# Patch embedding of an audio tower: one fp32 product of normalised patches becomes three fp32r products of raw patches, with the norm applied behind them

## The reference

```python
def layer_norm(x, gamma, beta, eps):
    mu = jnp.mean(x, axis=-1, keepdims=True)
    var = jnp.mean(jnp.square(x - mu), axis=-1, keepdims=True)
    return (x - mu) * jax.lax.rsqrt(var + eps) * gamma + beta

x = layer_norm(x, g1, b1, 1e-6)                # x: (64, 7, 1024)
x = jnp.einsum('bpd,dh->bph', x, W) + b        # W: (1024, 512)
h = layer_norm(x, g2, b2, 1e-6)
h = h + attention(layernorm(h))                # 16 heads of 128
h = h + ffn(layernorm(h))                      # inputs rounded to fp8, 512 x 512
```

## Time and profile before

| | us |
|---|---|
| median of 3 runs | 274.49 |
| lowest and highest | 274.19 and 275.79 |
| the profiled execution | 274.52 |
| its span in the trace | 272.7 |

### The profile page before, as it was taken

One profiled execution on the slowest core, in us unless ns is written; L12 is line 12 of the kernel. 1 busy time (PEld: TensorE's weight loads), 2 busy tenths in 40 slices (PEclk: granted clock), 3 DMA queues, 4 the chain that ended last, 5 costly groups with the idle time before them and its releaser, 6 DMA issues.

```text
span 272.7 us, 3956 instructions
## 1 busy us (share of the span) xinstructions
PE 264.4 (97%) x1506; PEld 225.6 (83%) x1506; DVE 156.6 (57%) x325; ACT 129.5 (47%) x220; POOL 0.2 (0%) x4
## 2 busy tenths in 40 slices
PE   6899999999999999999999999999999999999995
PEld 6434446999999999999999999999999999988963
DVE  4579878555545536264555445363555454578892
ACT  2664952364535443544435344445545354356460
POOL 0000000000000000000000000000000000000000
PEclk9999999999999999999999999999999999999999
DMA  6999000124314040413223040404133100000004
GB/s 169 335 288 394 6 0 1 54 102 154 101 55 154 0 154 0 154 19 135 58 96 132 22 154 0 154 0 154 19 135 95 59 0 0 0 4 0 0 2 135
DMA packets 5444, 23.82 MB, mean 87 GB/s; under 512 B 1019, under 2 KB 1483, under 8 KB 3260
## 3 DMA queue, kind: packets, MB, share of 16 engines
q1 hardware_dynamic: 5436, 23.71, 25.9%
HBM read 22.79 MB, written 0.92 MB: 87 GB/s over the span
## 4 chain that ended last, share of the span: by engine, by line
PE 92%; DVE 3%; DMA 2%; SPq 1%; ACT 1%; issue 1%; DVEq 0%
PE bank L274 15%; PE bank L275 15%; PE bank L276 15%; PE acc L309 10%; PE acc L411 8%; PE bank L387 5%; PE bank L395 5%; PE acc L415 4%; PE bank L401 2%; PE acc L524 2%; PE bank L380 2%; DMA tokw_raw<-tok_w 2%; PE bank L282 2%; PE acc L479 1%; PE acc L494 1%; SPq L228 1%
## 5 line engine op out<-in xcount | busy, mean ns | idle before, releaser
L274 PE MATMUL bank<-ht_hi,qkvw_hi 128*128 128x448 f32 (+2 forms) x204 | 74.7, 366 | 0.5 <-DVE ht_lo L749 0.5
L275 PE MATMUL bank<-ht_lo,qkvw_hi 128*128 128x448 f32 (+2 forms) x204 | 73.3, 359 | 0.0
L276 PE MATMUL bank<-ht_hi,qkvw_lo 128*128 128x448 f32 (+2 forms) x204 | 73.2, 359 | 0.0
L749 DVE TENSOR_TENSOR qkvw_lo<-raw,qkvw_hi 128x1536 fp32r<-128x1536 f32 x16 | 28.1, 1758 | 30.7 <-ACT qkvw_hi L546 30.7
L274 PEld LDWEIGHTS bank<-ht_hi,qkvw_hi 128*128 128x128 f32 x204 | 38.4, 188 | 3.7 <-issue 0.6
L276 PEld LDWEIGHTS bank<-ht_hi,qkvw_lo 128*128 128x128 f32 x204 | 38.3, 188 | 3.3
L275 PEld LDWEIGHTS bank<-ht_lo,qkvw_hi 128*128 128x128 f32 x204 | 38.4, 188 | 3.0
L749 DVE TENSOR_TENSOR z_lo<-bank,z_hi 128x448 fp32r<-128x448 f32 x15 | 9.4, 624 | 43.2 <-ACT z_hi L546 43.2
L309 PE MATMUL acc<-tokw_raw,xt 128*112 128x512 f32 x64 | 29.3, 598 | 0.9 <-DMA tokw_raw<-tok_w 0.9
L546 ACT CAST qkvw_hi<-raw 128x1536 fp32r<-128x1536 f32 x16 | 23.6, 1482 | 0.0
L309 PEld LDWEIGHTS acc<-tokw_raw,xt 128*112 128x112 f32 x64 | 10.6, 176 | 14.1 <-issue 9.6
(11 more groups left out here) (122 smaller groups left out, 355.8 us busy)
## 6 DMA issues: line engine op xcount, KB each, us to landing
raw<-heads_w SPq DMA_DIRECT2D x16, 1024.0 KB, 4.9
tokw_raw<-tok_w SPq DMA_DIRECT2D x4, 512.0 KB, 6.9
x_in<-patches SPq DMA_DIRECT2D x3, 448.0 KB, 8.7
ffnw_raw<-ffn_w SPq DMA_DIRECT2D x1, 1024.0 KB, 18.5
out<-h_sb SPq DMA_DIRECT2D x3, 224.0 KB, 2.3
x_in<-patches SPq DMA_DIRECT2D x2, 224.0 KB, 3.0
g_row<-tok_g SPq DMA_DIRECT2D x1, 224.0 KB, 11.2
b_row<-tok_b SPq DMA_DIRECT2D x1, 224.0 KB, 11.6
```

The costliest lines, as they stand in the source:

```text
L274: nc.tensor.matmul(ps, hi, whi, start=first, stop=False, skip_group_check=True)
L275: nc.tensor.matmul(ps, hi, wlo, start=False, stop=False, skip_group_check=True)
L276: return nc.tensor.matmul(ps, lo, whi, start=False, stop=last, skip_group_check=True)
L749: return nc.vector.tensor_tensor(dst, src, hi.bitcast(F32), ALU.subtract)
```

## The change

The transposes now take the raw patches. With s the standard deviation of a row and m its mean, the normalised product is (x·g1)W/s - (m/s)·(g1 W) + b1 W + b. The second norm doesn't care about a factor common to a row, so the kernel computes s times that: (x·g1)W - m·(g1 W) + s·(b1 W + b), and adapts the epsilon of the next norm.

- `patch_full` brings the raw transposed block out times g1 (`x_full`, on DVE for tiles 0 and 1, on ACT for tiles 2 and 3), `patch_hi` casts it on ACT, and the low part is taken on DVE for tiles 0 and 1 and on GpSimd for tiles 2 and 3.
- The weights are split: `split_tokw` casts each piece on ACT, `tokw_lo_part` takes the low part on GpSimd. `embed` issues three fp32r products where there was one in fp32.
- Two spare columns of tile 0's patches hold g1 and b1, so that rows 112 and 113 of `acc[0]` become g1 W and b1 W (+ b, added by `gains_done`). They are split into `gain_rows` (`gains_hi`, `gains_lo`).
- The row statistics (-m and s) of two tiles at a time go into `stat_cols`, are transposed (`stat_transposes`) and split into `stat_t`, and one product a tile, `recentre`, adds them and ends the tile (`tok_ps`).
- The unpaired Newton iterations are gone: each inverse root starts from a square root on ACT (`token_root`, `stream_root`). The low part of the first head's weights moves from DVE to GpSimd. `tokw_raw` now lies in the two slots of `raw`, so that the heads' first loads wait for the last low part of the weights, and `x_full` lies in `ffnw_raw`.

```diff
@@ SP: loads
+            load_tokw(0)
             load(x_in[:, 1, :], patches[1], x_landed[1])
-            load_tokw(0)
...
+            sp.wait_ge(tokw_lo_ok, len(TOKW_PIECES))
             for s in range(2):
                 sp.dma_start(raw[:, s, :], heads_w[s]).then_inc(raw_landed[s], 16)
+            sp.wait_ge(x_lo_late_ok, 4)
             sp.dma_start(ffnw_raw[:], ffn_w).then_inc(ffnw_landed, 16)
@@ PE
+            def embed(t, piece):
+                a, b = TOKW_PIECES[piece]
...
+                pe.wait_ge(x_hi_ok, 2 * t + half + 1)
+                pe.wait_ge(tokw_hi_ok, piece + 1)
+                for k in range(a, b):
+                    nc.tensor.matmul(acc[t][0:m, :], xt_hi[:, t, k, 0:m], tokw_hi[:, k, :], start=(k == 0),
+                                     stop=False, skip_group_check=True)
...
+                for k in range(a, b):
+                    nc.tensor.matmul(acc[t][0:m, :], xt_lo[:, t, k, 0:m], tokw_hi[:, k, :], start=False,
+                                     stop=False, skip_group_check=True)
+                pe.wait_ge(tokw_lo_ok, piece + 1)
+                for k in range(a, b):
+                    nc.tensor.matmul(acc[t][0:m, :], xt_hi[:, t, k, 0:m], tokw_lo[:, k, :], start=False,
+                                     stop=False, skip_group_check=True)
+            def gains_done():
+                pe.wait_ge(tok_b_lo_ok, 1)
+                nc.tensor.matmul(acc[0][0:SPARE, :], bias_row[:], tok_b_split[:], start=False, stop=False,
+                                 skip_group_check=True).then_inc(gain_ps, 1)
+            def recentre(t):
+                pe.wait_ge(gain_lo_ok, 1)
+                pe.wait_ge(stat_lo_ok, t // 2 + 1)
+                nc.tensor.matmul(acc[t][0:TR, :], stat_t[:, t, :], gain_rows[:], start=False, stop=True,
+                                 skip_group_check=True).then_inc(tok_ps, 1)
...
+            embed(0, 0)
+            embed(0, 1)
+            patch_transposes(1)
+            embed(0, 2)
+            embed(1, 0)
+            embed(0, 3)
+            gains_done()
+            stat_transposes(0)
+            patch_transposes(2)
+            embed(1, 1)
+            recentre(0)
+            embed(1, 2)
+            patch_transposes(3)
+            embed(1, 3)
+            recentre(1)
+            stat_transposes(1)
+            for piece in range(4):
+                embed(2, piece)
+            recentre(2)
+            stream_transposes(0)
+            embed(3, 0)
+            embed(3, 1)
+            stream_transposes(1)
+            embed(3, 2)
+            embed(3, 3)
+            recentre(3)
             stream_transposes(2)
@@ ACT
-            take_root(0)
-            normalise(0, slice(IN_DIM // 2, IN_DIM))
...
+            patch_hi(0, 0)
+            patch_hi(0, 1)
+            split_tokw(0)
+            split_tokw(1)
+            patch_hi(1, 0)
+            patch_hi(1, 1)
+            split_tokw(2)
+            split_tokw(3)
...
@@ GpSimd
+            tokw_lo_part(0)
+            tokw_lo_part(1)
+            tokw_lo_part(2)
+            tokw_lo_part(3)
+            b = slice(B_LO, B_LO + 1)
+            pool.wait_ge(tok_b_hi_ok, 1)
+            pool.wait_ge(tokw_lo_ok, len(TOKW_PIECES))
+            lo_part(tok_b_split[b], tok_b_raw[b], tok_b_split[b]).then_inc(tok_b_lo_ok, 1)
+            pool.wait_ge(tok_b_lo_ok, 1)
+            for t in range(2, TILES):
+                for half in range(2):
+                    patch_lo(t, half)
+            pool.wait_ge(qkvw_hi_ok, 1)
+            lo_part(qkvw_lo[0][:].rearrange("p a k e -> p (a k e)"), raw[:, 0, 0:QKV],
+                    qkvw_hi[0][:].rearrange("p a k e -> p (a k e)")).then_inc(qkvw_lo_ok, 1)
@@ DVE
+            patch_full(0, 0)
+            patch_full(0, 1)
+            patch_lo(0, 0)
+            patch_lo(0, 1)
+            patch_moments(0)
+            patch_full(1, 0)
+            patch_full(1, 1)
+            patch_lo(1, 0)
+            patch_lo(1, 1)
+            patch_moments(1)
+            patch_sigmas(0)
+            patch_moments(2)
+            stat_lo(0)
+            patch_moments(3)
+            gains_lo()
+            patch_sigmas(1)
             dve.wait_ge(rows_landed, 32)
-            stream_norms(0, None, patch=(3, patch_moments(3)))
-            stream_norms(1, 0)
-            stream_norms(None, 1, between=lambda i: split_qkv(0, 0) if i == 0 else None)
-            stream_norms(2, None, between=lambda i: stream_lo(0) if i == 0 else None)
-            stream_norms(None, 2)
-            stream_lo(1)
-            stream_norms(3, None, between=lambda i: stream_lo(2) if i == 0 else None)
-            stream_norms(None, 3)
+            stream_norms(0, between=lambda: stat_lo(1))
+            stream_norms(1, between=lambda: stream_lo(0))
+            stream_norms(2, between=lambda: stream_lo(1))
+            stream_norms(3, between=lambda: stream_lo(2))
             stream_lo(3)
```

More of the change, by code:

```diff
@@ L288, in patch_transposes @@
                     pe.wait_ge(ident_landed, 16)
-                    pe.wait_ge(x0_half_normed, 1)
-                else:
[L291 to L315, removed]
+                pe.wait_ge(x_landed[t], 16)
@@ new lines, in patch_full, with split_tokw @@
+            def patch_full(t, half):
+                act.wait_ge(xt_ps, 2 * t + half + 1)
+                act.wait_ge(x_lo_ok, 2 * (t - 2) + half + 1)
+                for k in range(half * HALF, (half + 1) * HALF):
+                    last = nc.scalar.mul(x_full[:, t % 2, k, :],
+                                         bank[2 * (t % 2) + half][:, k % HALF * TR:(k % HALF + 1) * TR],
+                                         g1_col[:, k:k + 1])
+                last.then_inc(x_full_ok, 1)
+            def split_tokw(i):
+                a, b = TOKW_PIECES[i]
+                act.wait_ge(tokw_landed[i], 16)
+                hi_part(tokw_hi[:, a:b, :], tokw_raw[:, a:b, :]).then_inc(tokw_hi_ok, 1)
@@ new lines, in gains_hi, with token_root @@
+            def gains_hi():
+                act.wait_ge(gain_ps, 1)
+                for row in (G_ROW, G_AGAIN):
+                    hi_part(gain_rows[row:row + SPARE - G_ROW, :], acc[0][G_ROW:SPARE, :]).then_inc(gain_hi_ok, 1)
+            def token_root(t):
+                c = TILES + t
+                act.wait_ge(tok_var_ok, t + 1)
+                act.wait_ge(x_eps_ok, t // 2 + 1)
+                nc.scalar.activation(root[:, c:c + 1], moments[:, c, 1:2], ACT.Sqrt, bias=x_eps_4[:, t:t + 1],
+                                     scale=4.0).then_inc(tok_root_ok, 1)
@@ L571, in normalise_stream, with stream_root @@
+            def stream_root(t):
+                c = 2 * TILES + t
+                act.wait_ge(h_var_ok, t + 1)
+                nc.scalar.activation(root[:, c:c + 1], moments[:, c, 1:2], ACT.Sqrt, bias=eps_4[:, 1:2],
+                                     scale=4.0).then_inc(h_root_ok, 1)
             def normalise_stream(t):
@@ new lines, in moments_of, with rsqrt_from_root @@
+                nc.vector.bn_aggr(moments[:, c, :], stats[:, c, 0:len(parts), :]).then_inc(done, 1)
+            def rsqrt_from_root(c, minus_v4):
+                v, y, n = vscaled[:, c:c + 1], rstd[:, c:c + 1], newton[:, c:c + 1]
+                link(nc.vector.reciprocal(y, root[:, c:c + 1]))
+                need(minus_v4)
+                link(nc.vector.scalar_tensor_tensor(out=n, in0=y, scalar=v, in1=y, op0=ALU.mult, op1=ALU.mult))
+                link(nc.vector.scalar_tensor_tensor(out=y, in0=n, scalar=3.0, in1=y, op0=ALU.add, op1=ALU.mult))
```

387 lines of the change are left out of this document (220 added, 167 removed).

## The result

The changed kernel takes 289.67 us (median of 4 runs, 286.26 to 290.13), against 274.71 for the kernel before beside it (274.19 to 275.79). The ratio is 1.050, with a 95% interval from 1.046 to 1.054; the quotient of the two medians alone is 1.054. The profiled execution took 290.13 us, with a span of 288.3: 15.6 more than the 272.7 before.

A forecast was written before the change was run, and what follows sets the result against it. PE bounded the kernel before; after the change, queues of GpSimd, ACT and DVE would. S at 29.8 plus 23.75 puts Q at 53.6 against 45.06, so 274.5 + 8.5 = 283 us, range 278 to 289.

The forecast's parts named there:

- PE's work: Ahead of the head loop: products cost 24.4 us instead of about 31, 6.6 less, but PE doesn't stay the bound.
- S: Start of DVE's norms of tile 0, forecast at 29.8 us against 20.5 before.
- steps 1 to 3: Ahead of S: tile 0's start, GpSimd's low parts of pieces 0 and 1, then pieces 2, 3 and bias up to `recentre`.
- Step 1: PE's warm-up ends at 5.85 us, tile 0's transposes start there; PE's first product stays at 9.4, nothing won.
- From S to Q: Norm pairs one tile at a time on DVE, with waits for ACT's roots of 1.4 and 0.9 us: 23.75 us.
- Q: Start of the first head's queries and keys, forecast at 53.6 us against 45.06; everything behind it unchanged.
- Its own signs of being wrong: First statistics of `acc[0]` before 24 us, DVE's waits on GpSimd showing in the norms, or a differing head loop.
- GpSimd at DVE's pace: Rival on GpSimd's low parts: each piece costs 1.22 us less, S 25.9, Q 49.7, 279 us; chance 0.16.
- No change: Rival on the path to Q: S near 24 with no waits on ACT, 273 to 277 us; chance 0.07.
- faster: Rival: the norms start as early as before, at 20.5 us, Q 41.9, 271.3 us; chance 0.07.
- Exclusion: Rival: DVE operations with two SBUF inputs wait for a whole GpSimd operation; Q 57.8, 287 us; chance 0.22.
- clock: Rival: PE's idling drops it to 1.2 GHz, 3.7 us behind Q, up to 2 before S; 288 us; chance 0.10.

The follow-up runs named there:

- e2: The changed kernel with products of ones that nobody reads in PE's gaps: 285.69 us, 1.040 of the kernel before.
- e1: The changed kernel with GpSimd's low part of the first head's weights cut into 12 instructions of 128x128: 287.14 us, 1.044 of the kernel before.
- e8: The changed kernel with all engines' orders rewritten, fillers, and every low part of weights and bias on DVE: 273.99 us, 0.9955 of the kernel before.
- e10: e8 with each of GpSimd's four late low parts of the patches as four instructions of 128x112: 273.38 us, 0.9934 of the kernel before.
- e7: The changed kernel with all engines' orders rewritten and fillers, GpSimd keeping three of four weight pieces: 280.02 us, 1.016 of the kernel before.

## Why the prediction was right, and where its size was off

The direction held: slower, by 5%. The range held only just: over the 274.5 of before, 278 to 289 is 1.013 to 1.053, and the ratio of 1.050 lies inside, but the median of 289.67 stands 0.7 us above its upper end. The single value of 283 was 5 to 7 us short.

- **PE's work, and that it is not the bound**: right at the full clock. The products cost 0.23 us each there, and PE was idle for 2.6, 2.5 and 5.4 us ahead of its waits. The gain of 6.6 us on PE shows nowhere. At half the clock PE did become the bound for a time, from 22.66 to 28.8 us.
- **The path to S**, steps 1 to 3: right in GpSimd's prices (2.35 for 2.44, 1.27 for 1.37, 3.48 for 3.5) and, with the clock held (e2), in its last links over GpSimd and the bias to the gains. As the kernel ran, PE's slow products had taken the place of GpSimd's second piece and of the bias. S was 4.1 us later. Step 1 took the start of the warm-up from the earlier trace rows and missed that `ones_ok` is now raised by GpSimd, which costs 0.5 us; the warm-up itself took 0.9 longer, and its length, from 4.69 to 5.57 us between executions, is explained by no edit. So the transposes came 1.3 us late (7.16 for 5.85 on the chain). With the clock held S is 30.39, 0.6 over the forecast, about what the held `sigma_num` costs.
- **From S to Q**: 25.8 for 23.75. The two waits for roots on ACT were there, but cost 0.80 and 0.71 us where 1.4 and 0.9 were forecast. The norm pairs of tiles 1 and 2 took 5.36 us each without their waits, for the forecast's 5.6 and, on tile 1, 0.2 more. The exclusion costs 3.4 (0.51 on tile 1, 2.93 on tile 2), which e1 gives back in good part. So the terms at hand were 1.4 too high together, and hid a part of the one left out.
- **Q as the only thing that moves**: 0.9 us short, the head's first products at 1.2 GHz. Only the first six of them ran slow, where the rival had priced 24 with 3.7 us.
- **Its own signs of being wrong**: one came true. DVE's waits on GpSimd show in the norms, though in the step `newton` and not in the write of `h_sb`, where the rival had looked for it.
- **The rivals**: *GpSimd at DVE's pace* fell by the first row. *No change* and *faster* fell with S at 33.94. *Exclusion* and *clock* are both true. The weak step is in how the numbers follow: the two were given chances as cases that exclude each other, each on top of the plain sum, and so the value forecast left both out. Exclusion alone was priced at 4 us and clock alone at 5. They touch different engines and places, so both together had to be a case with a chance of its own, at some 283 + 4 + 5 = 292. It came to 289.7.

By the Trainium skill (SBUF — State Buffer, Who interferes with whom) whoever issues first keeps the shared ports for its whole instruction, and the other fully blocks. The runs agree, both ways: 3.15 us for 0.22 on DVE, 2.68 for 1.27 on GpSimd. The same section counts `tensor_scalar` among the operations that can take both ports, given the right operands. `x_eps`, a TENSOR_SCALAR with one input from SBUF, took 1.28 us under GpSimd and 0.16 in e8; the RECIPROCAL and the statistics of the patches beside it were not held.

## What to carry to other kernels

When several mechanisms in the profile can each make a change slower and touch different engines, price them together; as rivals that shut each other out, they hide the case in which several hold. Before moving work to GpSimd, list the DVE instructions with two SBUF inputs (and the likes of `x_eps`) that will stand beside it: each, however small, may wait for a whole GpSimd instruction, and the trace shows that inside its duration, not as idle time. A saving on the engine that bounds a stretch is worth what the next engine's queue allows. Here the same arithmetic was 5% slower or 0.7% faster by placement, order, the size of GpSimd's instructions and fillers alone. And before you read an edit's worth from one execution, see how far the same code moves without it: S moved by 2.5 us here.

## What the runs showed of the hardware

- GpSimd's subtraction of two SBUF inputs took 2.35 us for 128x1024, 3.48 for 128x1536, 1.06 for 128x448, against 1.23, 1.75 and 0.62 on DVE: 1.7 to 2 times, near the 1.96 that the Trainium skill (GPSIMD Engine Reference, Performance versus the Vector engine) gives for an addition of two fp32 inputs. In instructions of 128x128 it took 0.46 each.
- The granted clock fell to about half after PE had been idle for 2.6 us at 8.0 us, and the products of 0.23 us took 0.43. Products of ones in the gaps, which do nothing for the result, kept it at 1.00 and took 4 us off the time of the changed kernel.
- The runs spread less with fillers: 3.9 us for the changed kernel, 1.1 for e2, 1.0 for e10. That this is the clock's doing isn't shown: the ten runs of e8, with fillers, spread over 2.3 us, and those of e7, whose clock fell to 0.78, over 0.5.
